# A graph layer kernel: at most three gathers in flight, the sort's tables in PSUM, and eight tiles finished by rows

## The reference, cut to what matters

```python
w_m = (efeat @ W_msg + b_msg).reshape(E, 16, 16)
w_a = (efeat @ W_attn + b_attn).reshape(E, 16, 16)
h = feat[src][:, :, None]
e1, e2 = w_m * h, w_a * h
ex = exp(e2 - segment_max(e2, dst)[dst])
ft = segment_sum(e1 * ex / segment_sum(ex, dst)[dst], dst).sum(axis=1)
x = layernorm(x + ft)
x = layernorm(x + segment_sum(efeat, dst) / max(counts, 1))
```

## Time and profile before

| | |
|---|---|
| median of three runs | 2309.12 us |
| the profiled execution | 2309.43 us |
| its span, first to last instruction | 2307.6 us |
| mean granted TensorE clock | 0.946 of full |
| first gather starts, last gather starts | 31.8, 2215.6 us |
| last product of TensorE ends | 2286.3 us |
| last scatter starts | 2295.51 us |

### The profile page before, as it was taken

How to read it: one execution, slowest core, us unless ns; L and a number is a source line. 1 busy time by engine, 2 the same in 40 slices (tenths; PEclk the granted TensorE clock), 3 DMA queues, 4 the chain that set the end, 5 groups by cost and what they waited for, 6 DMA issues and landing times.

```text
span 2307.6 us, 21909 instructions
## 1 busy us (share of the span) xinstructions
PE 2005.4 (87%) x6784; PEld 911.8 (40%) x6784; DVE 1867.7 (81%) x2922; ACT 1306.8 (57%) x1241; POOL 1682.1 (73%) x1748
## 2 busy tenths in 40 slices
PE   2548889998999998899989898899989898998886
PEld 0313334443444444444444443344444443444432
DVE  5557777987888988888987887798878887888886
ACT  6425545655566556665655755565556565565552
POOL 5777777777777777777777777777777777777740
PEclk8758999999999999999999999999999999999998
DMA  6100011001100001000100110101001010110110
GB/s 232 55 13 13 13 15 19 7 13 18 13 12 13 13 13 17 12 12 13 17 12 12 17 12 12 17 12 16 12 12 16 12 15 12 15 15 11 14 27 9
DMA packets 60072, 46.93 MB, mean 20 GB/s; under 512 B 28526, under 2 KB 55679, under 8 KB 59436
## 3 DMA queue, kind: packets, MB, share of 16 engines
q0 software_dynamic: 57776, 29.87, 9.3%
q1 hardware_dynamic: 2172, 15.58, 1.9%
HBM read 44.01 MB, written 1.23 MB: 20 GB/s over the span
## 4 chain that ended last, share of the span: by engine, by line
PE 36%; POOL 30%; issue 14%; DVE 14%; DMA 2%; ACT 2%; POOLq 0%; DVEq 0%; SPq 0%; ACTq 0%
POOL AR L624 29%; PE PX L1048 28%; PE PW L1034 7%; DVE AR L1348 7%; DVE AR L1361 3%; PE PTB L1023 2%; DVE AR L1378 1%; DMA AR<-in_xt,AR 1%; POOL AR L642 1%; DVE AR L1365 1%; POOL y_d L657 1%; DMA AR<-in_dst,QI 1%; ACT PX L881 0%; DVE AR L1379 0%; DMA AR<-in_es,AR 0%
## 5 line engine op out<-in xcount | busy, mean ns | idle before, releaser
L624 POOL DMA_INDIRECT AR<-in_xt,AR x1628 | 1572.2, 966 | 501.0 <-issue 486.6
L1048 PE MATMUL PX<-AR,CS 128*128 128x512 f32 x3304 | 1583.4, 604 | 6.8 <-ACT AR L825 6.6
L1348 DVE CUSTOM_DVE_ANT_1 AR<-PW,AR 128x1024 f32<-128x1024 f32 x826 | 987.7, 1220 | 183.0 <-PE PW L1034 127.6
L1048 PEld LDWEIGHTS PX<-AR,CS 128*128 128x128 f32 x3304 | 633.7, 193 | 586.5 <-issue 462.6
L1034 PE MATMUL PW<-WS,LT 100*128 100x512 bf16 x1652 | 514.8, 398 | 204.0 <-DVE AR L1348 203.0
L1361 DVE TENSOR_TENSOR AR<-AR,PX 128x1024 f32<-128x1024 f32 (+1 forms) x448 | 508.2, 1134 | 74.3 <-ACT PX L881 47.7
L819 ACT ACTIVATE LT<-PTB 100x1024 bf16<-100x1024 bf16 (+1 forms) x224 | 214.3, 957 | 529.8 <-PE PTB L1023 529.8
L883 ACT ACTIVATE AR<-AR 128x2048 f32<-128x2048 f32 (+1 forms) x224 | 429.3, 1917 | 7.3
L887 ACT ACTIVATE PX<-AR 128x1024 f32<-128x1024 f32 (+1 forms) x224 | 217.2, 970 | 326.4 <-DVE AR L1361 323.6
L1034 PEld LDWEIGHTS PW<-WS,LT 100*128 100x128 bf16 x1652 | 144.9, 99 | 584.2 <-issue 290.0
L881 ACT ACTIVATE PX<-AR 128x1024 f32<-128x1024 f32 (+1 forms) x224 | 235.6, 1052 | 22.9 <-DVE AR L1361 21.3
(11 more groups left out here) (149 smaller groups left out, 481.8 us busy)
## 6 DMA issues: line engine op xcount, KB each, us to landing
AR<-in_xt,AR POOLq DMA_INDIRECT x1631, 2.3
AR<-in_ea SPq DMA_DIRECT2D x3, 3128.0 KB, 13.6
AR<-in_ea SPq DMA_DIRECT2D x1, 3120.0 KB, 10.2
AR<-in_es,AR POOLq DMA_INDIRECT x49, 3.5
y_d<-AR POOLq DMA_INDIRECT x49, 2.1
AR<-y_d SPq DMA_DIRECT2D x1, 784.0 KB, 4.6
CS<-in_cst SPq DMA_DIRECT2D x1, 442.0 KB, 5.1
AR<-in_xt SPq DMA_DIRECT2D x1, 392.0 KB, 3.1
```

The source lines that it names most:

```text
L624: g.indirect_dma_start(feat(h, j - j0, j - j0 + 1), None, xt, bass.IndirectOffsetOnAxis(ap=XE[:, at:at + 1], axis=0)).then_inc(hg_sem(h), 16)
L1048: i = pe.matmul(PDR, IDN, x, start=(a == 0 and j == 0), stop=(g == LAST[k] and j == n - 1))
L1348: v.tensor_tensor_reduce(em(g, j, j + 2).rearrange("p (x c) -> p x c", c=32), w, hb, 1.0, LOW, ALU.mult, ALU.max, accum_out=MXC[:, k % 2, ...
```

## The change

- At most `FLIGHT = 3` gathers are in flight: gather number x waits until number x-3 has landed. Three semaphores replace those by tile, and `landed` waits for all three.
- The edges of tile 0 are gathered ahead of `WRUN`. SP holds the first `features` load back until they have landed. `y_d` is filled with zeros once, in the head, from `OUTR`, which GpSimd clears there.
- The edge attributes for the squares come from a second, transposed input (`eat`), so ScalarE reads them in order; `squares(0)` stands behind the counts.
- `OH`, `DGC`, `QFR`, `KF`, `PK` and two more tables of the sort lie in PSUM. All permutations stand ahead of the last check.
- `MAIN = NC - 8`: tiles 0 to 40 go through `y_d`. Their normalization, `main(0)` to `main(13)`, stands on VectorE at the ends of steps 215 to 228. SP's loads wait for 41 scatters; `results` stops with tile 40, still behind the gathers of tile k+5.
- The last eight tiles keep their own order: six are normalized on GpSimd by 55 small operations, two by VectorE (`last_batch`); GpSimd scatters all eight.
- `pairs`: for four groups among the last eight steps VectorE adds slots pairwise, so that `gsum` has seven slots fewer in all.
- The ring has 64 slots instead of 66; two memsets of `XP` move from GpSimd to VectorE.

```diff
-MAIN = NC - 3
+MAIN = NC - 8
+REST = NC - MAIN
+BATCH = [(0, REST - 2), (REST - 2, REST)]
-RING = 66
+RING = 64
+FLIGHT = 3
+ADDS = [c for p, c in STEPS[-8:] if p is None]
...
+        def landed(e, g):
+            n = UPTO[g]
+            for i in range(FLIGHT):
+                e.wait_ge(d_h[i], 16 * ((n - i + FLIGHT - 1) // FLIGHT))
...
+            sp.wait_ge(d_xe[0], 16)
+            sp.wait_ge(S["g_m"], 9)
+            sp.dma_start(YD.rearrange("(p c) w -> p c w", c=NC), OUTR[:, :, :]).then_inc(S["d_yz"], 16)
             features(0)
-            sp.wait_ge(d_xe[0], 16)
+            sp.wait_ge(S["d_yz"], 16)
             features(1)
...
-                sp.wait_ge(S["d_y"], 16 * NC)
+                sp.wait_ge(S["d_y"], 16 * MAIN)
...
             def gather(k, h):
-                j0, n = GRP[h][1:3]
-                for j in range(j0, min(j0 + n, CAPS[k])):
+                j0, n = GRP[h][1], SLOTS[h]
+                for j in range(j0, j0 + n):
+                    x = UPTO[h] - n + j - j0
+                    if x >= FLIGHT:
+                        g.wait_ge(d_h[x % FLIGHT], 16 * (x // FLIGHT))
...
                 for k in range(1, NC):
                     feats(k)
-                    if k >= 5:
+                    if 5 <= k < MAIN + 5:
                         results(k - 5)
...
+                def pairs(g):
+                    half = GRP[g][2] // 2
+                    keep = KEPT(half)
+                    v.wait_ge(S["a_exp"], g + 1)
+                    v.wait_ge(S["v_gm"], 2 * g + 2)
+                    sums = em(g, half, 2 * half - keep)
+                    v.tensor_tensor(sums, sums, em(g, half + keep, 2 * half), ALU.add).then_inc(S["v_ad"], 1)
...
+                def main(x):
                     if x == 0:
...
                         v.wait_ge(S["d_xn"], 16)
                         v.wait_ge(S["d_yl"], 16)
                         link(v.tensor_tensor(XNN, XNN, YN[:, :, 0:16], ALU.add))
...
-                    if 0 <= i - USED[LAST[MAIN]] - 2 < 4:
-                        norms(i - USED[LAST[MAIN]] - 2)
-                    if i - 3 == USED[LAST[NC - 2]]:
-                        last(0, 2)
-                last(2, 3)
+                    if 0 <= i - USED[LAST[MAIN - 1]] - 5 < 14:
+                        main(i - USED[LAST[MAIN - 1]] - 5)
+                last_batch()
```

More of the change, by code:

```diff
@@ L638, in runs_of @@
                         g.wait_ge(S["a_p"], 4 * (k - 3) + 3)
-                        for h in range(FIRST[k - 3], LAST[k - 3] + 1):
-                            g.wait_ge(hg_sem(h), hg_count(h))
+                        landed(g, LAST[k - 3])
                     lo = xoff[k % 3]
@@ L676, in regular @@
                      .then_inc(S["d_xg"], 16)
[L677 to L686, removed]
+                done = [0]
@@ new lines, in regular @@
+                g.wait_ge(S["d_xg"], 16 * REST)
+                g.wait_ge(S["v_sa"], NC)
+                g.wait_ge(S["v_ln"], 1)
+                means = OUTR[:, MAIN:NC - 2, 16:32]
+                then(g.tensor_tensor(means, means, RCL[:, 0:REST - 2].unsqueeze(2).broadcast_to([128, REST - 2, 16]), ALU.mult))
+                for b, (lo, hi) in enumerate(BATCH):
+                    if hi < REST:
+                        g.wait_ge(S["a_out"], MAIN + hi)
+                        then(g.tensor_tensor(YS[:, lo:hi, :], XG[:, lo:hi, :], OUTR[:, MAIN + lo:MAIN + hi, 0:16], ALU.add))
+                        norm(lo, hi)
+                        then(g.tensor_tensor(YS[:, lo:hi, :], YS[:, lo:hi, :], means[:, lo:hi, :], ALU.add))
+                        norm(lo, hi)
+                    else:
+                        g.wait_ge(S["v_ys"], 1)
+                    if b == 0:
+                        g.wait_ge(S["d_out"], 48)
+                    for x in range(lo, hi):
+                        g.indirect_dma_start(out, bass.IndirectOffsetOnAxis(ap=NODE[:, MAIN + x:MAIN + x + 1], axis=0), YS[:, x, :], None)\
+                         .then_inc(S["d_ou"], 16)
@@ L808, in _ @@
             counts(0, len(BY_ACT))
+            squares(0)
             squares(1)
@@ L1327, in floors @@
                     k, j0 = GRP[lo][0:2]
-                    for g in range(lo, hi):
-                        v.wait_ge(hg_sem(g), hg_count(g))
+                    landed(v, hi - 1)
                     if lo == FIRST[k]:
@@ L1465, in regular @@
                         gm(c, 1)
+                        if c in ADDS:
+                            pairs(c)
                     if nx is not None:
@@ L1497, in general @@
                 v.wait_ge(d_xe[0], 16)
-                for h in range(SOON):
-                    v.wait_ge(hg_sem(h), hg_count(h))
+                landed(v, SOON - 1)
                 for g5 in range(10):
@@ L1837 @@
     arrays, args = {}, []
-    for name, a in (("xt", xt), ("dst", dstp), ("src", srcp), ("ea", eap), ("es", es), ("wc", wc), ("cst", cst), ("cst2", cst2)):
+    for name, a in (("xt", xt), ("dst", dstp), ("src", srcp), ("ea", eap), ("eat", eat), ("es", es), ("wc", wc), ("cst", cst), ("cst2", cst2)):
         a = np.ascontiguousarray(a)
```

287 lines of the change are left out of this document (161 added, 126 removed).

## The result

The changed kernel takes 2369.27 us (median of 4 executions, 2368.58 to 2370.0) beside 2309.47 us of the kernel before (4 executions, 2309.01 to 2312.15). The ratio is 1.0257, with a 95% interval from 1.0239 to 1.0274: slower, 7 us above the forecast and inside its range. The profiled execution took 2369.81 us, its span is 2368.0 us, its mean granted clock 0.937.

A forecast was written before the change was run, and what follows sets the result against it. GpSimd's back-to-back gathers set the pace, the consumers alone the end after the last tile's edges. 2309.4 + 65.3 - 9.5 + 13 - 11.3 - 6 + 0 + 1.3 = 2362.2 us, 2% slower; range 2344 to 2382.

The forecast's parts named there:

- Term 1: VectorE at main(0), end of step 215, stands waiting for two loads behind the 41st scatter: +65.3 us.
- Term 6: Outside the head, the limit of three gathers in flight costs 0: landings take at most 3.8 us, met waits are free.
- Term 5: Head: first gather at 19.8 us, 11 us of stalls gone, 17.5 us lost to the limit: -6 us (-13 to +3.5).
- Terms 2 and 3: Consumers' waits for gathers vanish after the stand, -9.5 us; norms on VectorE in steps 216 to 228 add +13 us.
- Term 4: Step 229 to the last product: VectorE loses 19.4 us of norms, pairs take 6.1 us off TensorE: -11.3 us.
- Term 7: Last tiles: two scatters instead of one behind the last product's chain, GpSimd's small operations hidden: +1.3 us.
- (a): Rival: GpSimd is two tiles ahead when VectorE reaches step 215, so the wait is met: 2296 us, faster; chance 0.07.
- (b): Rival: the limit costs on every gather, 81 us for each 0.05 us in the gap: 2443 us; chance 0.07.
- (c): Rival: the head gives nothing, as gathers beside the loads fall further back: +3.5 instead of -6, 2372 us; chance 0.12.
- (d): Rival: GpSimd's norms end last, if its small operations take above 0.39 us each: 2375 us; chance 0.08.

The follow-up runs named there:

- the version with both edits: The changed kernel with main(0) to main(13) at steps 223 to 236 and FLIGHT = 8: 2282.14 us, ratio 0.9882 to the kernel before.

## Why the prediction was right, step by step

The sum was 2362.2 us; the profiled execution took 2369.8. The mechanism that it forecast, and its sign, are what the runs show: one wait that costs more than the whole change. That the sum comes within 8 us is in part luck, since 13.1 us that the head and the main part lost beyond the forecast stand against 6.1 us less behind step 229.

- **Term 1, the wait, +65.3.** Right. The place of the wait, two tiles ahead of the 41st scatter, is the cause: eight steps later it is gone, four steps later it is half, and with eight gathers in flight it is as long as with three. The chain behind the scatter was forecast at 2.1 + 0.4 + 4.6 + 1.0 us, and was 2.16 + 0.37 + 4.72 + 0.97.
- **Term 6, the limit of three elsewhere, 0.** Mis-sized. It costs 5 to 8 us in the main part by the gaps that a landing ended, and none with four. The satisfied waits are free, as the prediction read them off `runs_of` (with four in flight no gap of the main part is above 0.32 us); but 15 to 22 gathers did wait. The prediction compared the longest landing, 3.8 us, with the 3.75 us after which the third behind starts, and took the 0.05 us for nothing. In the changed kernel one gather starts at 717.99 with a wait of 1.65 us, 5.1 us after the third before it (gathers at 715.40 and 714.14, one each 1.25 us before that). The landing view shows no such gather, 2.5 us at most between 700 and 740 us and 4.0 us up to result 40, so the time until the engine goes on is longer than the view's landing. Why, no run shows. The rest of the 9.7 us by which the main part got longer up to result 40 is gathers that lasted longer, 27.2 us over 0.947 each instead of 25.5, and scatters of 1.00 instead of 0.98 us. That first sum varies from 24 to 34 us between the profiled executions on the first two chips, with no clear relation to the limit.
- **Term 5, the head, −6.** Mis-sized, it was −2.6. The first gather was forecast at 19.8 and came at 19.58 (of the 12.0 us taken off, the rows named give 9.4 and 2.15, not "about 2.6"). Stalls of 11 us were forecast to go; 9.3 came back with the tables in SBUF. The limit beside the loads was put at 17.5 us and took 20.0. So 19.6 + 60 + 20.0 + 0.9 for one long gather = 100.5, measured 100.37, instead of 97.3.
- **Terms 1, 5 and 6 together.** Result 40 was scattered at 2130.8; the prediction's 2123.7 − 6 is 2117.7. These 13.1 us are 3.4 of the head and 9.7 of the main part. The stand and its addition took 63.3 us where term 1 had 65.3, because VectorE too got there later (2075.7 instead of 2066.6 − 6).
- **Terms 2 and 3, steps 216 to 228.** 112.8 − 9.5 + 13 = 116.3 was forecast and 116.5 measured. VectorE is busy for 110.7 of it. GpSimd's waits at `runs_of(47)` and `runs_of(48)` were 2.4 and 3.5 us, where 5 and 4 were forecast, and hidden. The run with the norms eight steps later bears on both terms: it gained 54 us, and 65.3 − 9.5 is 55.8.
- **Term 4, step 229 to the last product.** 96 us forecast, 93.2 measured. TensorE was busy for 89.3 of it, not 93.1, and its gaps took 3.9 us, not 3. Over the whole run it has 14 matmuls less (6784 to 6770) and is busy 6.3 us less (2005.4 to 1999.1), close to the 6.1 forecast for the pairs; this stretch has 27 matmuls less, so some of the work of before lies ahead of it now. How much of the 14.1 us is due to the pairs and how much to VectorE's lighter steps is not shown.
- **Term 7, the last tiles.** +1.3 us was forecast; behind the last product the span has 19.3 us instead of 21.3. The last scatter starts 9.2 us after that product, as before: the last norms were over 1.3 us sooner, which pays for the second scatter. The other 2.0 us lie behind the start of the last scatter (10.1 us to the end of the span instead of 12.1); no run shows why. GpSimd's norms are hidden, as forecast, but barely. Their first and last operation, the first scatter, and the two last scatters of the changed kernel:

```profile
2328.80 0.35 POOL L718 TENSOR_TENSOR AR<-AR 128x96 f32<-128x96 f32 x1 [52.10 <-ACT AR L871]
...
2347.84 0.35 POOL L708 TENSOR_TENSOR AR<-AR 128x96 f32<-128x96 f32 x1
2348.60 1.07 POOL L727 DMA_INDIRECT out<-AR  x1 [0.41 <-POOL AR L708]
...
2356.63 0.96 POOL L727 DMA_INDIRECT out<-AR  x1 [0.38 <-DVE AR L1517]
2357.89 0.95 POOL L727 DMA_INDIRECT out<-AR  x1 [0.30 <-issue]
```

54 operations take 19.4 us with their gaps (18 us were forecast), 0.36 us each, where 0.39 was the point at which they would end last. The 0.38 us in front of the seventh scatter is hardly more than the gap of 0.30 us that each has. In the version with both edits that point is passed: there `main(13)` comes later, GpSimd starts its norms at 2243.62 behind VectorE's L1467, and its eight scatters follow each other without waiting for VectorE.

Added up: 2362.2 + 13.1 + 0.2 − 2.8 − 3.3 = 2369.4, and 0.4 us is left.

**The rivals.** (a), the wait is met, did not happen. (b), the limit costs on every gather: not on every one, but the row that spoke against it only showed that met waits are free. (c), the head gives nothing (+3.5): not so, but −2.6 us lies between it and the forecast's −6. (d), GpSimd's norms end last: missed by less than 0.1 us. The ends of the step terms, added up straight, give 2349 to 2380 us, not 2350 to 2374; the range stated holds both.

## What to carry to other kernels

Before an operation with a wait is put into an ordered list of steps, look up in the trace when its data lands and when its engine reaches the step: the difference is paid nearly in full when the engine feeds the others, and four more steps of distance were worth 27 us here. A limit on transfers in flight costs nothing only if it is above the longest landing time divided by the issue time, with a margin (here 4.0 us over 1.25 us is 3.2: three cost 5 to 8 us in the main part, four nothing); where big loads run beside the transfers it needs its own number from that stretch. The gains of several edits made together (here 26 us, which both repairs bring out) can hide behind one misplaced wait and one limit set too low.

## What the runs showed of the hardware

**TensorE after a stand.** The mean granted clock was 0.52, close to the lower of its two levels (1.2 GHz), over the 61 us in which TensorE had nothing to do (third column from the right in the windows of the changed kernel). The first four products of `gsum` after it took 3.06 us, the next four 1.89:

```profile
2140.34 1.03 PE L1081 MATMUL PW<-WS,LT 100*128 100x512 bf16 x2 [63.88 <-DVE AR L1404]
2141.17 3.06 PE L1101 MATMUL PX<-AR,CS 128*128 128x512 f32 x4
2144.06 0.59 PE L1081 MATMUL PW<-WS,LT 100*128 100x512 bf16 x2
2144.50 1.89 PE L1101 MATMUL PX<-AR,CS 128*128 128x512 f32 x4
```

The lower clock after the stand costs under 2 us in these rows.

**GpSimd's small operations.** Six elements per partition take 0.20 us and 96 take 0.35. The same operation on 12 elements took 0.22 us, and 1.18 us when VectorE added two SBUF operands beside it. Timelines of GpSimd and of VectorE in the version with both edits:

```profile
2247.17 1.18 POOL L693 TENSOR_TENSOR AR<-AR 128x12 f32<-128x12 f32 x1
...
2250.58 0.22 POOL L693 TENSOR_TENSOR AR<-AR 128x12 f32<-128x12 f32 x1
```

```profile
2247.06 1.23 DVE L1425 TENSOR_TENSOR AR<-AR 128x1024 f32<-128x1024 f32 x1
```

**Landing beside loads gets longer with more in flight.** Gathers started between 19 and 60 us land in 7.1 us (median) with three in flight, 7.4 with four and 9.1 with eight; between 28 and 60 us one gather starts per 2.4, 1.9 and 1.4 us (30.9 us in 13, 31.1 in 16 and 31.1 in 22 steps).

**Two chips on which every kernel took about 3.2 ms.** The kernel before took 38 and 40% longer on the third and fourth chip. The operations of VectorE, ScalarE and GpSimd last as long as elsewhere (the product of L1404 1.22 us); TensorE is busy for some 2170 us instead of 1995, at a mean granted clock of 0.83 instead of 0.95. The rest is waiting that the profile can't attribute to an instruction of this core (it names the releaser "remote"): in the last run with fourteen in flight 1111 us in 66 waits of ScalarE's L861 and 962 us in 122 of VectorE's L1404, and up to 44.5 us at a time in the four runs. At the end of the run GpSimd's norms have their usual distances. What slows these chips is not known from these runs.

**Short dependent operations that start late.** In both runs with fourteen in flight, which both ran on these chips, many of VectorE's short operations that wait for each other start 1.40 us apart between 40 and 90 us. With eight in flight on the same two chips they follow each other as on the first chip. Timelines of VectorE, first the version with both edits on the first chip, then eight in flight without pairs on the fourth, then fourteen in flight on the fourth:

```profile
44.69 0.19 DVE L1291 TENSOR_SCALAR AR<-DG 128x49 f32<-128x49 f32 x1
44.91 0.20 DVE L1292 TENSOR_REDUCE NRM<-AR 128x1 f32<-128x49 f32 x1
```

```profile
46.65 0.19 DVE L1291 TENSOR_SCALAR AR<-DG 128x49 f32<-128x49 f32 x1
46.87 0.20 DVE L1292 TENSOR_REDUCE NRM<-AR 128x1 f32<-128x49 f32 x1
```

```profile
60.36 0.19 DVE L1291 TENSOR_SCALAR AR<-DG 128x49 f32<-128x49 f32 x1 [1.20 <-issue]
61.76 0.20 DVE L1292 TENSOR_REDUCE NRM<-AR 128x1 f32<-128x49 f32 x1 [1.21 <-issue]
```

The two kernels differ before the last steps only in the number in flight, so the late starts go with fourteen in flight and not with the chip alone; whether they would come on the first two chips, no run shows. The sort ends so late with them that GpSimd waits 38.6 and 35.0 us for it before the edges of tile 1, against 22.6 and 24.0 us with eight.

A ratio measured on these chips, 1.008 to 1.018, has another sign than the 0.988 of nearly the same kernel on the first chip, so a verdict between two kernels holds for chips of one pace only.
